# Splitting q on 128 partitions, and inverting softmax sums without their repeats, with DMA in between

## The reference

```
q = (x @ Wq).reshape(b, s, 32, 32)          # 32 heads of 32
k, v = split(x @ Wkv)                       # one key and one value head for all
scores = einsum('bqhd,bkd->bhqk', q, k) * 32 ** -0.5
scores = where(causal, scores + slope[h] * (key_pos - query_pos), -inf)
attn = softmax(scores)
out = einsum('bhqk,bkd->bqhd', attn, v) @ Wo
x = layernorm(x + out)
```

## Time and profile before

| | us |
|---|---|
| median of 3 runs | 4210.84 (4203.0 to 4215.06) |
| span of the profiled execution | 4202.6 |
| TensorE busy | 3850.6 (92%) |
| VectorE busy | 2472.1 (59%) |
| ScalarE busy | 1929.4 (46%) |
| GpSimd busy | 1359.6 (32%) |
| the 256 inversions (line 607) | 233.8 |
| the 256 copies of q's high part (line 481) | 150.0 |
| the 256 subtractions for its low part (line 582) | 176.0 |

### The profile page before, as it was taken

The page is one execution under the profiler, slowest core; times in us unless marked ns, Lnnn a source line. Parts: engine busy times, 40 slices in busy tenths (PEclk is TensorE's granted clock), DMA queues, the critical chain, the costliest instruction groups (busy, mean ns, idle before and its releaser), DMA issues. The chain is left out here.

```text
span 4202.6 us, 73921 instructions
## 1 busy us (share of the span) xinstructions
PE 3850.6 (92%) x22065; PEld 2340.6 (56%) x22065; DVE 2472.1 (59%) x4462; ACT 1929.4 (46%) x3253; POOL 1359.6 (32%) x420
## 2 busy tenths in 40 slices
PE   5989989999999998789999999999999599999998
PEld 3555544444444443555554444544443388888887
DVE  4566666666766672556666656766675244444444
ACT  2445645565666565344555656566565401000000
POOL 1114434444444454112433444445454200000010
PEclk8899989999999998899998999999998799999999
DMA  2111110000000001111001000000000311111111
GB/s 72 47 51 27 28 41 22 20 21 16 19 19 14 19 6 34 54 44 49 26 26 43 19 22 22 14 19 14 19 14 6 131 56 60 60 60 60 60 60 51
DMA packets 159069, 152.11 MB, mean 36 GB/s; under 512 B 8388, under 2 KB 141508, under 8 KB 156584
## 3 DMA queue, kind: packets, MB, share of 16 engines
q1 hardware_dynamic: 158696, 147.70, 11.9%
HBM read 96.75 MB, written 33.62 MB: 31 GB/s over the span
## 5 line engine op out<-in xcount | busy, mean ns | idle before, releaser
L509 ACT ACTIVATE prob<-ps_s,alibi 128x512 f32<-128x512 f32 (+3 forms) x2560 | 1524.5, 623 | 1193.3 <-PE ps_s L774 603.4
L589 DVE TENSOR_REDUCE mxp<-ps_a 128x1 f32<-128x512 f32 (+3 forms) x2560 | 1457.6, 605 | 910.2 <-PE ps_a L707 462.5
L452 POOL TENSOR_TENSOR prob<-prob 128x2048 f32<-128x2048 f32 (+1 forms) x240 | 1043.8, 4349 | 1298.2 <-ACT prob L509 1298.2
L771 PE MATMUL ps_s<-qst,kexp 97*128 97x512 f32 (+3 forms) x2560 | 1107.2, 444 | 84.8 <-ACT prob L509 52.8
L771 PEld LDWEIGHTS ps_s<-qst,kexp 97*128 97x128 f32 x2560 | 504.1, 198 | 905.9 <-ACT prob L509 710.4
L707 PE MATMUL ps_a<-kmax,qst 97*128 97x512 f32 (+3 forms) x2560 | 950.3, 397 | 29.2 <-DMA qst<-qst 13.4
L794 PE MATMUL ps_o<-prob,val 128*32 128x512 f32 (+3 forms) x5120 | 624.8, 562 | 0.0
L707 PEld LDWEIGHTS ps_a<-kmax,qst 97*128 97x128 f32 x2560 | 503.3, 197 | 107.6 <-DVE mxp L589 52.7
L794 PE MATMUL ps_sum<-prob,ones 128*32 128x512 f32 (+3 forms) x3200 | 384.8, 569 | 0.1
L980 POOL TENSOR_TENSOR hb_sb<-h_sb,bias_b 128x1024 f32<-128x1024 f32 x32 | 76.9, 2402 | 790.9 <-DVE z_sb L1124 731.1
L607 DVE RECIPROCAL r_sb<-s_sb 128x128 f32<-128x128 f32 x256 | 233.8, 931 | 122.0 <-ACT s_sb L515 119.8
(11 more groups left out here) (148 smaller groups left out, 3672.5 us busy)
## 6 DMA issues: line engine op xcount, KB each, us to landing
wq_raw<-in_L_attn_Wq SPq DMA_DIRECT2D x65, 512.0 KB, 3.8
xs<-in_L_attn_hidden_states SPq DMA_DIRECT2D x9, 2048.0 KB, 8.1
qst<-qst SPq DMA_DIRECT2D x64, 256.0 KB
att_scratch<-at_sb SPq DMA_DIRECT2D x64, 256.0 KB, 2.3
at_raw<-att_scratch SPq DMA_DIRECT2D x32, 512.0 KB, 5.4
x_sb<-in_L_attn_hidden_states SPq DMA_DIRECT2D x32, 512.0 KB, 4.3
out<-z_sb SPq DMA_DIRECT2D x32, 512.0 KB, 3.1
z_sb<-in_L_attn_Wo SPq DMA_DIRECT2D x4, 512.0 KB, 5.3
```

Of the source, the lines that this page charges most:

```text
L452: nc.gpsimd.tensor_tensor(even[:, :, c1:], even[:, :, c1:], odd[:, :, c1:], ALU.add).then_inc(pair_done, 1)
L509: nc.scalar.activation(prob[slot][:, h, c0:], ps_s[bank][:, c0:], ACT.Exp, bias=alibi_of(u, h, k - QT * s)).then_inc(e_done, 1)
L589: nc.vector.tensor_reduce(mxp[:, h * QT + t, c:c + 1], ps_a[bank][:, 0:cols], AX.X, ALU.max).then_inc(a_done, 1)
L771: last = nc.tensor.matmul(ps_s[bank][:, c0:], kexp[0:KR, k * P:(k + 1) * P], qst[buf][0:KR, h, c0:], start=True, stop=not diagonal)
```

## The change

For q: after the projection ScalarE copies all 128 rows of `ps_m` at once into a new tile `qhw` (four heads by 32 rows), and VectorE subtracts all 128 rows at once into `qlw`. SP then stacks them into `qst` by 12 DMAs of 32 rows by 512 elements: two for the high part of each head, one for its low part. "QE" is one entry in the list, at the place of its first head.

For the sums: part 0 of "R" is a DMA of four rows of `s_sb`, one for each head, to `sum_rows` in DRAM. Part 1 brings them back as 128 x 16 elements. At part 2 VectorE inverts these, and a DMA writes them to `rec_rows` in DRAM. Part 3 is four DMAs, each of which reads one row and writes it to 32 partitions of `r_sb`. Part 4 is the multiplication and the store as before. The table of places is not changed.

```diff
-        misc += [(min(s + 1, 3), ("QE", h)) for h in range(GH)]
+        misc += [(GH * min(s + 1, 3), ("QE", 0))]
...
             def repeat_q(b, s, u, buf):
                 g = unit_no(b, s, u)
-                sp.wait_ge(ql_done, START + GH * (g + 1))
-                sp.dma_start(qst[buf][DH:2 * DH].bitcast(F32), qst[buf][0:DH].bitcast(F32)).then_inc(stack_in, 16)
+                sp.wait_ge(qh_done, START + g + 1)
+                for h in range(GH):
+                    head = slice(h * DH, (h + 1) * DH)
+                    for r in range(2):
+                        sp.dma_start(qst[buf][r * DH:(r + 1) * DH, h].bitcast(F32),
+                                     qhw[head].bitcast(F32)).then_inc(stack_in, 16)
+                sp.wait_ge(ql_done, START + g + 1)
+                for h in range(GH):
+                    head = slice(h * DH, (h + 1) * DH)
+                    sp.dma_start(qst[buf][2 * DH:3 * DH, h].bitcast(F32), qlw[head].bitcast(F32)).then_inc(stack_in, 16)
...
+            def recip_part(g, part):
+
+                if part == 0:
+                    sp.wait_ge(o_copied, START + 2 * g)
+                    sp.wait_ge(s_part, START + 16 * (g - 1))
+                    sp.dma_start(sum_rows, s_sb[::DH]).then_inc(s_row, 16)
+                elif part == 1:
+                    sp.wait_ge(s_row, START + 16 * g)
+                    sp.wait_ge(rec_done, START + g - 1)
+                    sp.dma_start(sum_c[:], sum_rows.rearrange("h (j e) -> (h j) e", j=DH)).then_inc(s_part, 16)
+                elif part == 2:
+                    sp.wait_ge(rec_done, START + g)
+                    sp.wait_ge(r_in, START + 16 * GH * (g - 1))
+                    sp.dma_start(rec_rows.rearrange("h (j e) -> (h j) e", j=DH), rec_c[:]).then_inc(r_row, 16)
+                elif part == 3:
+                    sp.wait_ge(r_row, START + 16 * g)
+                    sp.wait_ge(at_done, START + g - 1)
+                    for h in range(GH):
+                        sp.dma_start(r_sb[h * DH:(h + 1) * DH],
+                                     rec_rows[h].partition_broadcast(DH)).then_inc(r_in, 16)
+                else:
+                    store_before(g)
...
             def divide(g):
 
-                pool.wait_ge(r_done, START + QT * g)
+                pool.wait_ge(r_in, START + 16 * GH * g)
+                pool.wait_ge(o_copied, START + 2 * g)
...
-            def take_q(number, buf, old_tiles, heads=range(GH)):
-                for h in heads:
-                    if h == 0:
-                        act.wait_ge(q_ps, START + 1 + number)
-                        act.wait_ge(s_full, old_tiles)
-                    nc.scalar.activation(qst[buf][0:DH, h], ps_m[h * DH:(h + 1) * DH], ACT.Copy,
-                                         scale=SCALE).then_inc(qh_done, 1)
+            def take_q(number):
+                act.wait_ge(q_ps, START + 1 + number)
+                act.wait_ge(stack_in, START + STACK * number)
+                nc.scalar.activation(qhw[:], ps_m[:], ACT.Copy, scale=SCALE).then_inc(qh_done, 1)
...
                     if what == "OE":
                         act.wait_ge(sm_done, steps + ktiles(s))
                         act.wait_ge(at_done, START + g)
+                        act.wait_ge(s_row, START + 16 * g)
...
-            def divide(g, part):
-
-                cols = slice(part * P, (part + 1) * P)
-                dve.wait_ge(o_copied, START + 2 * g)
-                dve.wait_ge(at_done, START + g - 1)
-                nc.vector.reciprocal(r_sb[:, cols], s_sb[:, cols]).then_inc(r_done, 1)
+            def invert(g):
+
+                dve.wait_ge(s_part, START + 16 * g)
+                dve.wait_ge(r_row, START + 16 * (g - 1))
+                nc.vector.reciprocal(rec_c[:], sum_c[:]).then_inc(rec_done, 1)
...
-                    if what == "R" and arg < QT:
-                        divide(g, arg)
+                    if what == "R" and arg == 2:
+                        invert(g)
```

More of the change, by code:

```diff
@@ L158, in program @@
     slope_rows = nc.dram_tensor("slope_rows", (NH, QB), F32, kind="Internal").ap()
+    sum_rows = nc.dram_tensor("sum_rows", (GH, QB), F32, kind="Internal").ap()
+    rec_rows = nc.dram_tensor("rec_rows", (GH, QB), F32, kind="Internal").ap()
     xb = x.rearrange("b (s t p) d -> b s p t d", t=QT, p=P)
@@ L177, in program, with attention @@
         ident = sb(ctx, "ident", [P, P], F32)
-        attention(nc, sb, pb, sem, slopes, xb, wq_v, wkv, att, slope_rows, ident)
+        attention(nc, sb, pb, sem, slopes, xb, wq_v, wkv, att, slope_rows, sum_rows, rec_rows, ident)
         feed_forward(nc, sb, pb, sem, xt, ot, wo_v, w_v, bias, la, lb, gate_w, gate_b, att, ident)
-def attention(nc, sb, pb, sem, slopes, xb, wq_v, wkv, att, slope_rows, ident):
+def attention(nc, sb, pb, sem, slopes, xb, wq_v, wkv, att, slope_rows, sum_rows, rec_rows, ident):
     with ExitStack() as ctx:
@@ L212, in attention @@
         qst = [sb(ctx, f"qst{i}", [P, GH, QB], F32R) for i in range(3)]
+        qhw = sb(ctx, "qhw", [P, QB], F32R)
+        qlw = sb(ctx, "qlw", [P, QB], F32R)
         mxp = sb(ctx, "mxp", [P, GH * QT, NSEG], F32)
@@ L221, in attention @@
         r_sb = sb(ctx, "r_sb", [P, QB], F32)
+        sum_c = sb(ctx, "sum_c", [P, GH * QB // P], F32)
+        rec_c = sb(ctx, "rec_c", [P, GH * QB // P], F32)
         at_sb = sb(ctx, "at_sb", [P, QB], F32)
@@ L273, in attention @@
         o_copied = counter("o_copied")
-        r_done = counter("r_done")
+        s_row = counter("s_row")
+        s_part = counter("s_part")
+        rec_done = counter("rec_done")
+        r_row = counter("r_row")
+        r_in = counter("r_in")
         at_done = counter("at_done")
@@ L286, in attention @@
         UB = NSEG * HG
+        STACK = (1 + 3 * GH) * 16
         def walk(eng, prologue, unit_step, epilogue):
@@ L392, in step @@
                 for what, arg in plan:
-                    if what == "R" and arg == QT:
-                        store_before(unit_no(b, s, u))
-                    if what == "QE" and arg == GH - 1:
+                    if what == "R":
+                        recip_part(unit_no(b, s, u), arg)
+                    if what == "QE":
                         repeat_q(b, s2, u2, parity(s, const + 2))
@@ L402, in epilogue @@
                 load_x(b, NSEG, (b + 1) % B)
-                store_before(b * UB + UB)
+                for part in range(QT + 1):
+                    recip_part(b * UB + UB, part)
             sp.dma_start(xs[:], xb[0, 0]).then_inc(x_in, 16)
@@ L577, in take_v, with take_q @@
                     "p (t d) -> p t d", t=QT)).then_inc(vt_done, 1)
[L579 to L584, removed]
+            def take_q(g):
+                dve.wait_ge(qh_done, START + g + 1)
+                nc.vector.scalar_tensor_tensor(qlw[:], ps_m[:], SCALE, qhw[:].bitcast(F32), ALU.mult,
+                                               ALU.subtract).then_inc(ql_done, 1)
             def maximum(tiles, i, chunk, bank):
@@ L613, in prologue @@
                 take_v(b, 0)
-                take_q(b * UB, 0)
+                take_q(b * UB)
                 for i, chunk in enumerate(a_chunks(0)):
                     maximum(START + b * TILES_B, i, chunk, bank_of(i))
-                take_q(b * UB + 1, 1)
+                take_q(b * UB + 1)
                 shifts(b * UB, START + b * TILES_B, 0, 0)
@@ L637, in step @@
                         shifts(g + 1, tiles + GH * ktiles(s), *ahead(s, u, 1, const))
-                    if what == "R" and arg < QT:
-                        divide(g, arg)
+                    if what == "R" and arg == 2:
+                        invert(g)
             def epilogue(b):
-                for part in range(QT):
-                    divide(b * UB + UB, part)
+                invert(b * UB + UB)
             walk(dve, prologue, step, epilogue)
```

16 lines of the change are left out of this document (8 added, 8 removed).

## The result

The changed kernel takes 4445.21 us (median of four runs, 4427.18 to 4445.81) against 4209.77 (4203.0 to 4215.06) for the kernel before beside it. The ratio is 1.0548, 95% interval 1.0524 to 1.0571. It is slower by 5.5%; forecast were 2.6%.

The account below looks back on a forecast made before the run. TensorE was taken to bound the kernel, so only its idle time counts. Losses of 71 + 36 + 31 + 4 + 5 less 35 saved make 112 us; on 4202.6 this gives 4315, stated as 4320, range 4240 to 4475.

Parts of the forecast that it names:

- tails: Segments 1 to 3, from end of `shift_t` cast to start of `ps_o` copy: longer stretches lose 71 us, bounds 47 and 123.
- clock: Unit boundaries, segments 1 to 3: 26 shorter tails each lose 1.4 us once to TensorE's slow clock; 36 us, bounds 0 and 112.
- segment 0: SP's order there delays the shift: unit 26.3 us against 23.75, 2.55 more for each of 12; 31 us, bounds 0 and 63.
- prologues: Before the first maximum, 8.6 us from q against 6.7 of waiting: 4 us over both, nothing to 6.
- end of attention: Before feed-forward, the last `at_sb` takes 10.3 us against 5.0: 5 us, bounds 4 and 8.
- saved: Segments 1 to 3: fewer q activations and subtractions save 0.8 us in each of 44 units; 35 us, bounds 0 and 53.
- Sum 7.4 us: Segments 1 to 3, chain from cast through inversion, DMAs and multiplication: shortest possible tail 7.4 us, bounds 6.6 and 8.7.
- my own rule of differences: Segments 1 to 3: each tail loses chain length less old length; 17 of about 4.3 us, 9 of 5.7, 14 of 7.2.
- heavier case: Rival, chance 0.17: trips land at upper bounds and the clock falls twice at every boundary; 272 us more, 4475.
- my own (4320): Own case, chance 0.64: the sum of terms, 112 us more, stated as 4320 us, own range 4240 to 4430.
- evacuation case: Rival, chance 0.08: ScalarE and VectorE limit where q is taken; removed work saves 229 against losses of 147; 4121 us.
- nearly hidden case: Rival, chance 0.11: trips at lower bounds, no new clock fall, segment 0 covered, 53 saved; 3 us more, 4206.

Follow-up runs that it names:

- q_only: Kernel before with only the q half of the change; the sums are inverted as before. 4171.73 us, ratio 0.9921.
- bcast1: Changed kernel with part 3 as one DMA of 128 rows in place of four of 32. 4520.25 us, ratio 1.0719.
- fill: Changed kernel with unread matmuls at the start of each unit, 12 in segments 1 to 3 and 20 in segment 0. 4400.80 us, ratio 1.0454.
- sums_only: Kernel before with only the sums half of the change; q is taken head by head as before. 4334.99 us, ratio 1.0300.
- seg0_early: Changed kernel with only segment 0's places moved: sums chain ahead of the stack, multiplication behind the shift. 4334.85 us, ratio 1.0271.
- store13: Changed kernel with only segment 0's multiplication and store moved from place 9 to 13, behind the shift's DMA. 4405.59 us, ratio 1.0449.
- early: Changed kernel with only the table of places changed: parts early in each unit, multiplication behind the shift. 4173.03 us, ratio 0.9920.
- turn_fill: Changed kernel with six unread matmuls ahead of the turn of the shift in each unit. 4468.89 us, ratio 1.0599.
- q_fill: Kernel before with only the q half, plus six unread matmuls ahead of the turn of the shift. 4117.27 us, ratio 0.9756.

## Why the forecast was right in direction and wrong in size

What held: TensorE's idle time was the right thing to count; the place of the cost (ScalarE's copy behind `at_sb`, and the shift behind the store in segment 0); no tail of 4.3 us is left, the shortest in segments 1 to 3 is 7.3; the heads of q off the evacuation give something like 35 us (38 in q_only). What failed, by the terms of the sum:

| term | forecast | measured | how measured |
|---|---|---|---|
| tails | +71 | +102 | segments 1 to 3 of the table above without the row below: from a unit's cast to the next first score matmul, and from a unit's first to its third |
| clock | +36 | +70 | the rest of those units, from the third score matmul to the cast, changed kernel less q_only |
| segment 0 | +31 | +86 | table above |
| prologues | +4 | +19 | before the first score matmul, and between the batches |
| end of attention | +5 | +10.5 | behind the last "OE" |
| saved | -35 | -47 | the same rest, q_only less before |
| sum | +112 | +240.5 | the difference of the two spans |

*The tails.* The step that failed is "Sum 7.4 us". The chain's steps, as means over the 46 tails from the end of the cast: DMA out issued at 1.17 (I had 0.6), landed 1.49 us later (1.8 taken), first DMA in issued at 2.82, fourth 1.45 later (1.15 taken), landed 2.35 later (2.2), GpSimd's start at 6.88, its end at 8.15, the copy at 8.27 (its median is 8.21). The transfer out is shorter than I took it. SP is the slower part: after its DMA of the shift it comes to the DMA out 0.5 us later than I counted, and its three issues take 0.3 more. The fourth DMA lands in a median of 2.07, but in 14 of the 46 tails it takes 2.6 to 3.4. The sum is 0.8 us over mine, inside the bounds of 6.6 and 8.7, and at a chain of 8.2 my own rule of differences gives 17 x 3.9 + 9 x 2.5 + 14 x 1.0 = 103 us. Measured are 102 by the table, or 110 if one counts from each of the 46 casts to the next unit's third score matmul (480.4 against 370.5). So the mechanism was right and 0.8 us in a term that counts 40 times was 31 us. bcast1 answers in the same way: a tail 1.05 us longer, 75 us more.

*The clock.* The step was "I let each lose 1.4 once: 36 us". The rest of a unit, from the third score matmul to the cast, sums to 2223.2 us before, 2176.7 in q_only, 2247.0 in the changed kernel and 2177.1 in fill. Since q_only and the changed kernel share the work of that stretch except for the inversions, the 70 us between them are the price of what the wait leaves behind, and fill, which keeps TensorE busy in the wait, brings exactly that stretch back to q_only's. 70 us is twice what I took and inside my bound of 112. (Without the q half on either side it is 41: 2264.0 in sums_only less 2223.2.) The clock's mean in attention falls from 0.94 to 0.91. The Trainium skill (TensorE: Matmul & The Clock Gate, HAM oscillation) says that waits repeated in a loop cost the slow clock each time round; by that rule the long tails lose too. The trace agrees that TensorE falls back there each time, but it did so before the change, as I had argued when I set 20 us aside. From one cast to the next, at 44 boundaries, the time at the low level is this, in us:

| tails before | number | before | q_only | sums_only | changed kernel |
|---|---|---|---|---|---|
| 4.2 to 4.6 | 18 | 22 | 42 | 122 | 126 |
| 5.7 to 5.8 | 11 | 48 | 49 | 90 | 90 |
| 6.9 and more | 15 | 136 | 60 | 150 | 138 |

Against the kernel before, the new low clock (147 us) lies at the 29 short and middle tails. It is 5 us for each; at half the speed this is up to 2.5 us of work, by my estimate, where I had taken 1.4. Behind the long tails the change adds nothing to before, but it takes back what q_only alone had gained there (136 to 60): 25 of the 70 us lie behind them. The 70 us are not all to be had back: fill returns them in the rest of the units, but its own matmuls stand in front of the unit's first scores and lengthen the "tails" row by 44.

*Segment 0.* The step was "Sum 26.3, so 2.55 us more for each of 12 units". A unit lasts 31.3 us, not 26.3. Three parts: q is copied at 13.0 us instead of the 10.5 I took from the row at 139.73 (that row was an early one, the median before is 11.3, and "Q" itself now ends 1.8 us later, in a unit whose granted clock is 0.81); the twelve issues take 7.6 us, not 6.25, since behind one another a 64 KB transfer issues in a median of 0.59 and in up to 2.0 us instead of the 0.52 of one alone; and the rest, from the twelfth issue to the next unit, takes 10.1 us, not 8.95. I read the order of SP rightly, and it is what seg0_early and store13 confirm. It was also right to count both halves in one chain: sums_only alone is 12 us faster in this segment, q_only 3, both together 86 slower.

*Prologues and end.* The prologues' "0.6 + 12 x 0.52 + 1.8 = 8.6 us" is 9.9 each (row `ps_a` from `qlw`: 19.7 us over two, 13.4 before), and the first shift of each batch, which TensorE then waits for, stands behind the twelve issues (a wait of 8.3 to 8.4 us each, 2.3 before). The second batch's first unit starts later still: the stretch between the batches grows by 12 us, 6 of them in q_only alone and 7 in sums_only alone. I take the 7 for the last division of the first batch, which now takes a chain of trips. That I had called hidden. At the end, "Four trips (1.8 + 1.8 + 1.8 + 3.35)" missed what is queued ahead of them. SP's rows there:

```profile
3524.96 0.41 SPq L358 DMA_DIRECT2D xs<-in_L_attn_hidden_states  x1
3526.98 0.54 SPq L393 DMA_DIRECT2D sum_rows<-s_sb  x1
3532.66 0.35 SPq L397 DMA_DIRECT2D sum_c<-sum_rows  x1
...
3541.50 0.41 SPq L414 DMA_DIRECT2D att_scratch<-at_sb  x1
```

The 8 KB out, issued at 3526.98, release SP only 5.7 us later (1.8 to 1.9 in 30 of the other units). The 2 MB load of x, issued 2 us before them, lands at almost the same time, at 3532.8.

*The rivals.* The heavier case (4475) came closer than my own (4320), but not for its reasons as they stand: the trips stayed inside their bounds, and the clock's 70 us lie between my 36 and its 112. Segment 0, with 86, is over even the 63 of that case. The evacuation case was wrong in price, right in sign for its half: q_only gains 38 us, not 229. The nearly hidden case exists, as the kernel early, and not with this table. The Trainium skill (DMA: Bandwidth & Descriptors, Specifications) says that pieces under 512 bytes are not moved at line rate. By that rule the two transfers with pieces of 64 bytes would be longer; the trace does not agree, they land in 1.4 and 1.7 us (rows `rec_rows` and `sum_c` of the DMA issues), less than the 1.8 of the shift. No run moves the same bytes in longer pieces.

```profile
sum_c<-sum_rows SPq DMA_DIRECT2D x64, 8.0 KB, 1.7
rec_rows<-rec_c SPq DMA_DIRECT2D x64, 8.0 KB, 1.4
```

*The load.* "The DMAs add 0.5 MB to each unit" counts q alone; with the sums it is 0.8 MB, and in attention the mean rate goes from 27 to 40 GB/s (the 36 were the mean of the whole program). The landings in the chain stayed inside their bounds all the same.

**Open.** Why bcast1's one DMA kept so few engines busy. The halves' meeting in segments 1 to 3 (42 us): the changed kernel has the low clock of sums_only there, not that of q_only; that this eats the relief of q is argued, and no run shows it by itself. What the six products cost in turn_fill. Whether fill would give more with fewer matmuls.

## What to carry to other kernels

Moving work from an engine to DMA trades busy time, which may cost nothing, for latency, which costs wherever its end stands behind the last free place: 2 us of inversion became 8 us of trips, and the same instructions at an earlier place cost nothing. So when a step changes from short to long, its place in the order has to be chosen again, and the table of places belongs to the change. On a queue that works in order ask what stands behind the new DMAs, not only what they wait for: here the shift waited 8 us behind a chain and a store that it did not need. And two edits can cost more together than one by one (+90 us apart, +235 together) when they meet in one queue; a sum of terms needs a line for their meeting.

## What the runs showed of the hardware

- Six unread matmuls in a wait of 1 to 2 us, which TensorE meets once in every unit, took 54 us off 4171.7 (q_fill), with 154 us fewer at the low level (1.2 GHz) and the rest at 2.4 GHz. In the kernel whose tail is set by a chain of DMAs, the same six cost some 20 us (turn_fill).
- Twelve DMAs from SBUF to SBUF of 64 KB each, issued behind one another, took 7.6 us of SP's queue, and single issues up to 2.0 us; four that read DRAM take 1.7.
- One DMA that repeats four rows on 128 partitions (256 KB) released its reader 5.2 us after the issue, with at most 6 of its packets at a time; four DMAs for 32 partitions each did so in a median of 3.8 and a mean of 4.1, issues included, with up to 10 to 18 packets at a time.
- An 8 KB transfer issued 2 us after a 2 MB load on the same queue released its waiter after 5.7 us, when the load landed; in 30 other units it did so in 1.8 to 1.9.
